# One exponential over two PSUM banks instead of two over one each, and the diagonal key blocks first in the short query chunks, in the second attention of a transformer layer

## The chip, the cores and the metric

The kernel runs as one program on all 8 NeuronCores of one Trainium2 chip. Each core takes one sequence of the batch (4096 tokens of width 1024, float32) and no core talks to another. The time is that of the device, in microseconds, of the slowest core.

## The reference

What is computed, cut to its frame (`layernorm` before each stage, residual added after it):

```python
x = x + attn_a(layernorm(x))      # one head of width 1024, causal, softmax
x = x + ffn(layernorm(x))         # 1024 -> 64, 16 tiny relu units per channel, -> 1024
x = x + attn_b(layernorm(x))      # 16 heads of width 64, causal, then its own layernorm
x = x + ffn(layernorm(x))

# inside attn_b, for every head h
scores = q @ k.T                  # causal: key t is seen by query s only if t <= s
attn = softmax(where(causal, scores / sqrt(64), -inf))
out = attn @ v
```

## The kernel before

The program has four phases with a barrier between them: projections for attention A, attention A with its feed-forward part, projections for attention B (the keys and queries go to HBM, the values stay in SBUF as `v_sb`), and `phase_2b`, attention B with everything behind it. Only `phase_2b` is touched. It runs from about 2526 us to the end at 5371 us.

`phase_2b` works through eight chunks of 512 queries (`qc` 0 to 7). Query chunk `qc` sees `kcnt = 4*qc + 4` blocks of 128 keys (4, 8, ... 32 blocks); the last four of these lie on the diagonal and need a causal mask. In a chunk it goes through eight pairs of heads (`pr` 0 to 7). A head has 64 dimensions, so the two heads of a pair lie on partitions 0 to 63 and 64 to 127.

For every block of keys `kc` at position `pos` of the pair's loop:

- TensorE computes the transposed scores of both heads, 128 keys x 512 queries each, with two matmuls on 64 rows (L1262). They go to two neighbouring banks of `psQ`; `half = pos % 2` chooses banks 0 and 1 or banks 2 and 3. In the text these two are the "score matmuls".
- ScalarE takes the exponential of each head's bank (L1271) into one of three SBUF buffers `AP2[pos % 3]`. Before the change that is one instruction of 512 columns for each head, and the next score matmul on a bank waits only for the exponential that read this bank (`exp_done[(half, hh)]`).
- GpSimd, in the last four blocks only, zeroes what lies above the diagonal, with one `affine_select` for each head (L1280, the "mask"); it waits for both exponentials.
- TensorE multiplies the result with the values, one matmul for each head (L1238), and adds it up in `pc4` and `pc5` over all blocks (the "value matmuls"). These come two positions late in the order of TensorE's queue: scores of `pos`, then values of `pos - 2`. An extra column of ones in `v_sb` gives the sum of the weights in row 64.

After the loop comes the pair's end: Ln and Exp of the sums on ScalarE (L1299 to L1310), two broadcasts by matmul (L1316, L1321), and copies and products on VectorE (L1327 to L1339). The scores of the next pair's positions 0 and 1 are computed meanwhile, the second of them after the end's last VectorE product.

From chunk 1 on, the feed-forward and layernorm work of the chunk before is spread over the pairs by the list `pendf`: its piece `pr` is put into the queues behind the end of pair `pr`, and so runs in front of and beside the loop of pair `pr + 1`. Pieces 0 and 4 are `ep_lnb`: statistics on VectorE (L808, L811), a Ln and an Exp on ScalarE (L825, L828), and then, for each of two row tiles, one scaling (L840) and three adds or products of two SBUF tensors of 128x1024 float32 (L1411, L1414, L1417). Pieces 1 and 5 are statistics and two scalings (L840), pieces 2 and 6 a long chain of small VectorE operations (L903 to L916), pieces 3 and 7 the last matmul of the feed-forward part and, on GpSimd's queue, two stores to `out`. ScalarE's queue is in order, so the exponentials of the next pair stand behind the Ln and Exp of a piece. There is no `pendf` work in chunk 0.

Keys are loaded in pieces of 2048 (16 blocks); `npiece == 1` holds for the chunks with up to 16 blocks, 0 to 3.

Of the kernel before, what the change touches and what calls it, by code (L numbers as in the profile page):

```python
# [8 lines left out]
AF = mybir.ActivationFunctionType  # L9
# [88 lines left out]
def build_nc(debug=False):  # L98
# [27 lines left out]
    p = Prog()  # L126
# [10 lines left out]
    negC = e(nc.sbuf_tensor("negC", [128, 2], F32))  # L137
# [71 lines left out]
    psQ = e(nc.psum_tensor("psQ", [128, 2048], F32))  # L209
# [21 lines left out]
    sm = {n: Sem(e(nc.semaphore(n))) for n in sem_names}  # L231
    PE, DVE, SC, PL = sm["s_pe"], sm["s_dve"], sm["s_sc"], sm["s_pl"]
# [919 lines left out]
    def phase_2b():  # L1152
        exp_done = {}
# [12 lines left out]
        AP2 = [attb2[:, 0:2, :], attb2[:, 2:4, :],  # L1166
               k_sb.ap()[:, 5, 2048:3072].rearrange("p (a b) -> p a b", a=2)]
# [19 lines left out]
        for qc in range(NQ2):  # L1187
            q0 = qc * QC2
            kcnt = 4 * qc + 4
            npiece = (kcnt * 128 + 2047) // 2048  # L1190
# [35 lines left out]
            for pr in range(8):  # L1226
                if pr == 0:
                    issue_k_loads(0)
                def emit_av(kc, pos):
                    for hh in range(2):  # L1230
                        p.wait("tensor", SC, exp_at[kc])
                        if mask_at[kc]:
                            p.wait("tensor", PL, mask_at[kc])
                        if pos == 0:
                            p.wait("tensor", DVE, ctxn_dve[0])
                        h = 2 * pr + hh
                        att = AP2[pos % 3][:, hh, :]
                        p.op("tensor", lambda e_, hh=hh, kc=kc, h=h, att=att, pos=pos, kcnt=kcnt: e_.matmul(  # L1238
                            pb[4 + hh].ap()[0:65, :], v_sbB[:, kc, h, :],
                            att, start=(pos == 0), stop=(pos == kcnt - 1)),  # L1240
                            PE if hh == 1 else None)
# [1 line left out]
                exp_at = {}  # L1243
                mask_at = {}
                pend = []
                order = list(range(kcnt))
                seen_pc = set()
                for pos, kc in enumerate(order):
                    pc = (kc * 128) // 2048
                    koff = kc * 128 - pc * 2048  # L1250
                    half = pos % 2
                    ksl = kslot_of[(qc, pr, pc)]
                    if pc not in seen_pc:
                        seen_pc.add(pc)
                        p.wait("tensor", ksems3[ksl], ktgt[(qc, pr, pc)])
                    if pos == 1:
                        p.wait("tensor", DVE, max(ctxn_dve[0], opj23_free[0]))
                    pe_hh = {}
                    for hh in range(2):
                        bank = pb[2 * half + hh]  # L1260
                        p.wait("tensor", SC, exp_done.get((half, hh), 0))
                        p.op("tensor", lambda e_, b=bank, hh=hh, ks=kslots[ksl], koff=koff, pr=pr: e_.matmul(  # L1262
                            b.ap()[:, :], ks[hh * 64:(hh + 1) * 64, koff:koff + 128],
                            qb2[hh * 64:(hh + 1) * 64, pr, :],
                            start=True, stop=True, tile_position=(hh * 64, 0)), PE)
                        pe_hh[hh] = PE.n
                    for hh in range(2):
                        p.wait("scalar", PE, pe_hh[hh])
                        if pos % 3 == 0 and hh == 0:
                            p.wait("scalar", sm["s_cst"])  # L1270
                        p.op("scalar", lambda e_, ap=AP2[pos % 3], half=half, hh=hh: e_.activation(  # L1271
                            ap[:, hh, :],
                            psQ.ap()[:, half * 1024 + hh * 512:half * 1024 + (hh + 1) * 512],
                            AF.Exp, bias=negC.ap()[:, 1:2]), SC)
                        exp_done[(half, hh)] = SC.n
                    exp_at[kc] = SC.n
                    if kc >= kcnt - 4:
                        p.wait("gpsimd", SC)
                        for hh in range(2):
                            p.op("gpsimd", lambda e_, a_=AP2[pos % 3][:, hh, :], kc=kc, q0=q0: e_.affine_select(  # L1280
                                out=a_, in_=a_,
                                compare_op=ALU.is_ge, fill=0.0,
                                base=q0 - kc * 128, pattern=[[1, QC2]],
                                channel_multiplier=-1), PL)
                        mask_at[kc] = PL.n
                    else:
                        mask_at[kc] = 0
                    if len(pend) == 2:
                        emit_av(*pend.pop(0))
                    pend.append((kc, pos))  # L1290
# [4 lines left out]
                if pr < 7:  # L1295
# [5 lines left out]
                    bias=epsb.ap()[64:65, 2:3]), SC)  # L1301
                p.op("scalar", lambda e_: e_.activation(
                    NORM1[64:65, 0:512], pb[5].ap()[64:65, :], AF.Ln,
                    bias=epsb.ap()[64:65, 2:3]), SC)
# [149 lines left out]
    phase_a(True)  # L1454
    barrier()
    phase_2b()
    p.wait("sync", sm["s_stout"])
    p.wait("sync", sm["s_stx"])
# [56 lines left out]
```

## Time and profile before

| | us |
|---|---|
| median of 2 runs | 5377.53 (5365.68 to 5389.39) |
| the profiled execution | 5372.64 |
| its span on the slowest core (4) | 5371.0 |
| spans of all cores | 5348.1 to 5371.0 |

| engine, core 4 | busy us | share of the span |
|---|---|---|
| PE (TensorE matmul) | 3542.5 | 66% |
| ACT (ScalarE) | 2116.6 | 39% |
| DVE (VectorE) | 1682.5 | 31% |
| POOL (GpSimd) | 524.2 | 10% |

TensorE's granted clock over the whole span is 0.78 on every core; it goes between two levels, 0.5 (1.2 GHz) and 1.0 (2.4 GHz). These shares are means over four phases; the loop that is changed has other limits than the rest. The profile counts an engine as busy while any of its instructions is open, so an instruction that was handed to ScalarE early and waits inside for the one before it counts as busy too, and durations of ScalarE instructions in a dense row overlap. For the pace of such a row one reads the distance from start to start.

### The profile page before, as it was taken

The numbers are of one execution on the slowest core, as the hardware profiler recorded it, in microseconds if no ns is written. First come the engines' busy times: TensorE is split into PE (matmuls) and PEld (weight loads), VectorE is DVE, ScalarE is ACT, GpSimd is POOL, SyncE is SP. The second block draws the span as 40 slices with busy tenths as digits, with TensorE's granted clock in tenths as the row PEclk, the third lists the DMA queues.
The fourth block names the chain that finished last, engine by engine and source line by source line (L and its number), as shares of the span: only waits on it lengthen the run. The fifth ranks groups of instructions, "written<-read, shape, count | busy, mean of one in ns | idle before, by whom it ended". The sixth has DMA issues, their size and how long they took to land.

```text
span 5371.0 us, 49022 instructions; the slowest of 8 cores (5348.1 to 5371.0 us)
## 1 busy us (share of the span) xinstructions
PE 3542.5 (66%) x14217; PEld 1320.0 (25%) x14380; DVE 1682.5 (31%) x3093; ACT 2116.6 (39%) x3829; POOL 524.2 (10%) x916
## 2 busy tenths in 40 slices
PE   1157777567778577776555666677677777777872
PEld 1022222344555322222111111121122122122220
DVE  3222221433222343341144433323322322223126
ACT  0012223222222132222333554546656656757760
POOL 1100000000000010011211111111111001100100
PEclk9978888777888788887566767677788777887875
DMA  8723332111111134343001001010011011010000
GB/s 200 188 102 123 128 122 99 67 59 59 40 40 36 68 112 138 115 138 101 23 21 50 14 27 45 30 39 23 22 41 35 16 43 38 16 39 25 33 20 25
DMA packets 219381, 343.48 MB, mean 64 GB/s; under 512 B 88755, under 2 KB 119475, under 8 KB 219126
## 3 DMA queue, kind: packets, MB, share of 16 engines
q1 hardware_dynamic: 140198, 242.80, 13.7%
q0 software_dynamic: 25552, 80.76, 4.6%
q10 hardware_dynamic: 53376, 16.78, 1.3%
q8 instruction: 128, 2.10, 0.2%
q14 instruction: 127, 1.04, 0.1%
HBM read 260.60 MB, written 75.50 MB: 63 GB/s over the span
## 4 chain that ended last, share of the span: by engine, by line
PE 51%; DVE 18%; issue 9%; ACT 9%; DMA 8%; POOL 3%; DVEq 1%; SPq 0%; ACTq 0%; POOLq 0%
PE pc L1238 9%; PE psQ L684 8%; PE psQ L1262 8%; PE pc L724 5%; ACT arena_b L1271 4%; PE psQ L1068 4%; POOL arena_b L1280 2%; PE pc L1058 2%; PE psQ L1316 2%; DVE stat L811 2%; PE psQ L1321 2%; DVE arena_b L808 1%; DVE k_sb L808 1%; DVE stat L569 1%; ACT k_sb L1271 1%
## 5 line engine op out<-in xcount | busy, mean ns | idle before, releaser
L1271 ACT ACTIVATE arena_b<-psQ,negC 128x512 bf16<-128x512 f32 x1584 | 1003.2, 777 | 414.7 <-PE psQ L1262 357.5
L684 PE MATMUL psQ<-arena_b 128*128 128x512 bf16 x2000 | 567.7, 436 | 150.7 <-ACT arena_b L700 47.1
L1262 PE MATMUL psQ<-arena_b 64*128 64x512 bf16 x1528 | 489.2, 446 | 255.3 <-ACT arena_b L1271 181.8
L1238 PE MATMUL pc<-arena_b,v_sb 128*65 128x512 bf16 x1584 | 560.3, 440 | 108.3 <-POOL arena_b L1280 107.9
L1327 DVE COPY arena_f<-psQ 64x512 f32<-64x512 f32 x64 | 43.7, 682 | 1523.9 <-PE psQ L1316 1523.9
L1271 ACT ACTIVATE k_sb<-psQ,negC 128x512 bf16<-128x512 f32 x720 | 491.5, 790 | 12.3 <-PE psQ L1262 9.5
L1068 PE MATMUL psQ<-arena_b,k_sb 128*128 128x256 bf16 x2176 | 317.6, 296 | 26.4 <-ACT arena_b L1073 19.8
L1280 POOL TENSOR_SCALAR_AFFINE_SELECT arena_b<-arena_b 128x512 bf16<-128x512 bf16 x352 | 210.9, 625 | 1228.0 <-ACT arena_b L1271 1227.6
L1262 PE MATMUL psQ<-arena_b,k_sb 64*128 64x512 bf16 x776 | 248.0, 438 | 123.7 <-ACT arena_b L1271 94.2
L691 ACT ACTIVATE arena_b<-psQ 128x512 bf16<-128x512 f32 x256 | 152.6, 596 | 433.8 <-PE psQ L684 205.3
L724 PE MATMUL pc<-arena_b 128*128 128x512 bf16 x1000 | 251.1, 413 | 102.7 <-DMA arena_b<-wvB_s 53.5
L684 PEld LDWEIGHTS psQ<-arena_b 128*128 128x128 bf16 x2048 | 203.4, 108 | 465.5 <-issue 326.5
L1262 PEld LDWEIGHTS psQ<-arena_b 64*128 64x128 bf16 x1528 | 119.2, 95 | 743.0 <-issue 742.2
L1238 PE MATMUL pc<-k_sb,v_sb 128*65 128x512 bf16 x720 | 249.8, 432 | 44.7 <-POOL k_sb L1280 44.7
L1068 PEld LDWEIGHTS psQ<-arena_b,k_sb 128*128 128x128 bf16 x2176 | 228.8, 106 | 126.7 <-issue 38.7
L825 ACT ACTIVATE stat<-stat,epsb 128x2 f32<-128x2 f32 x48 | 14.2, 295 | 598.8 <-DVE stat L820 598.8
L532 DVE TENSOR_REDUCE nmax<-psQ 1x1 f32<-1x512 f32 x144 | 97.8, 679 | 469.8 <-PE psQ L665 290.7
L1073 ACT ACTIVATE arena_b<-psQ,negC 128x256 bf16<-128x256 f32 x272 | 124.9, 470 | 280.5 <-PE psQ L1068 280.5
L582 ACT ACTIVATE stat<-stat,epsb 128x4 f32<-128x4 f32 x16 | 4.8, 297 | 534.8 <-DVE stat L578 534.8
L1316 PE MATMUL psQ<-arena_f,ones_rowf 1*64 1x512 f32 x128 | 114.6, 993 | 146.5 <-ACT arena_f L1306 146.5
L1238 PEld LDWEIGHTS pc<-arena_b,v_sb 128*65 128x65 bf16 x1584 | 119.6, 117 | 357.9 <-issue 357.9
L1058 PE MATMUL pc<-v_sb,arena_b 128*128 128x512 bf16 x537 | 171.0, 385 | 6.7 <-issue 2.4
(173 smaller groups left out, 4077.0 us busy)
## 6 DMA issues: line engine op xcount, KB each, us to landing
arena_f<-x SPq DMA_DIRECT2D x64, 512.0 KB, 5.9
arena_f<-xs SPq DMA_DIRECT2D x64, 512.0 KB, 5.1
arena_b<-wkT_s SPq DMA_DIRECT2D x16, 1024.0 KB, 7.6
arena_b<-wqT_s SPq DMA_DIRECT2D x16, 1024.0 KB, 6.7
arena_b<-wvT_s SPq DMA_DIRECT2D x16, 1024.0 KB, 6.8
xs<-arena_f POOLq DMA_DIRECT2D x32, 512.0 KB, 3.8
arena_b<-wkB_s SPq DMA_DIRECT2D x16, 1024.0 KB, 7.3
arena_b<-wqB_s SPq DMA_DIRECT2D x16, 1024.0 KB, 7.4
```

The lines of the kernel that those rows point to most:

```text
L684: p.op("tensor", lambda e_, b=bank, ws=wslot, dc=dc, ec=ec: e_.matmul(b.ap()[:, :], wbuf[:, ws, dc % 4, ec * 128:(ec + 1) * 128], lnxT[:, ...
L691: p.op("scalar", lambda e_, b=bank, ec=ec: e_.activation(nsq[:, ec % 2, :], b.ap()[:, :], AF.Square), SC)
L724: p.op("tensor", lambda e_, b=bank, ws=wslot, dc=dc, kt=kt, oc=oc: e_.matmul(b.ap()[:, :], lnxT[:, dc, kt * 128:(kt + 1) * 128], wbuf[:, w ...
L808: p.op("vector", lambda e_, x=x, i=i, stv=stv: e_.scalar_tensor_tensor(junk_ap, x, 1.0, x, ALU.mult, ALU.mult, accum_out=stv[:, 2 + i:3 + ...
L1058: p.op("tensor", lambda e_, att=att, tch=tch, dh=dh, kc=kc, kcnt=kcnt: e_.matmul(AVB[tch][dh], att, v_sb.ap()[:, kc, dh * 512:(dh + 1) * 512],
L1068: p.op("tensor", lambda e_, b=bank, ec=ec, kc=kc, par=par: e_.matmul(b.ap()[:, 0:QS1], k_sb.ap()[:, ec, kc * 128:(kc + 1) * 128], qb1[:, e ...
L1073: p.op("scalar", lambda e_, b=bank, kc=kc: e_.activation(attT1[:, kc, :], b.ap()[:, 0:QS1], AF.Exp, bias=negC.ap()[:, 0:1]), SC)
L1238: p.op("tensor", lambda e_, hh=hh, kc=kc, h=h, att=att, pos=pos, kcnt=kcnt: e_.matmul(pb[4 + hh].ap()[0:65, :], v_sbB[:, kc, h, :], att, s ...
L1262: p.op("tensor", lambda e_, b=bank, hh=hh, ks=kslots[ksl], koff=koff, pr=pr: e_.matmul(b.ap()[:, :], ks[hh * 64:(hh + 1) * 64, koff:koff + ...
L1271: p.op("scalar", lambda e_, ap=AP2[pos % 3], half=half, hh=hh: e_.activation(ap[:, hh, :], psQ.ap()[:, half * 1024 + hh * 512:half * 1024 ...
L1280: p.op("gpsimd", lambda e_, a_=AP2[pos % 3][:, hh, :], kc=kc, q0=q0: e_.affine_select(out=a_, in_=a_, compare_op=ALU.is_ge, fill=0.0, base ...
L1316: p.op("tensor", lambda e_: e_.matmul(pb[2].ap()[0:64, :], ones_rowf.ap()[64:65, 0:64], YT[64:65, 512:1024], start=True, stop=True), PE)
```

## The change

Two edits in the loop over the key blocks of `phase_2b`:

1. The two exponentials of a block, 128x512 each, become one of 128x1024 that reads the two neighbouring banks. It waits for both score matmuls, and both score matmuls of the position two later wait for it (`exp_done[half]`).
2. In the chunks with `npiece == 1` (`qc` 0 to 3) the loop takes the last four blocks, the masked ones, first, and then the others. For chunk 0, which has only these four, the order stays what it was.

The masks, the value matmuls, their count, the pair's end and all other phases stay as they are.

```diff
-                order = list(range(kcnt))
+                if npiece == 1:
+                    order = list(range(max(0, kcnt - 4), kcnt)) + \
+                            list(range(0, max(0, kcnt - 4)))
+                else:
+                    order = list(range(kcnt))
...
+                    p.wait("tensor", SC, exp_done.get(half, 0))
                     if pos == 1:
                         p.wait("tensor", DVE, max(ctxn_dve[0], opj23_free[0]))
-                    pe_hh = {}
                     for hh in range(2):
                         bank = pb[2 * half + hh]
-                        p.wait("tensor", SC, exp_done.get((half, hh), 0))
                         p.op("tensor", ...)            # the score matmul
-                        pe_hh[hh] = PE.n
-                    for hh in range(2):
-                        p.wait("scalar", PE, pe_hh[hh])
-                        if pos % 3 == 0 and hh == 0:
-                            p.wait("scalar", sm["s_cst"])
-                        p.op("scalar", lambda e_, ap=AP2[pos % 3], half=half, hh=hh: e_.activation(
-                            ap[:, hh, :],
-                            psQ.ap()[:, half * 1024 + hh * 512:half * 1024 + (hh + 1) * 512],
-                            AF.Exp, bias=negC.ap()[:, 1:2]), SC)
-                        exp_done[(half, hh)] = SC.n
+                    p.wait("scalar", PE)
+                    if pos % 3 == 0:
+                        p.wait("scalar", sm["s_cst"])
+                    p.op("scalar", lambda e_, ap=AP2[pos % 3], half=half: e_.activation(
+                        ap[:, :, :],
+                        psQ.ap()[:, half * 1024:(half + 1) * 1024], AF.Exp,
+                        bias=negC.ap()[:, 1:2]), SC)
+                    exp_done[half] = SC.n
```

## Rows read from the trace of the kernel before

**Rows 1.** Chain of work that ended last: shares of the span by engine.

```profile
PE 51%; DVE 18%; issue 9%; ACT 9%; DMA 8%; POOL 3%; DVEq 1%; SPq 0%; ACTq 0%; POOLq 0%
```

**Rows 2.** Timeline, ScalarE, chunk 7: start us, length us, engine, line, operation, tiles, count.

```profile
4800.15 2.42 ACT L1271 ACTIVATE arena_b<-psQ,negC 128x512 bf16<-128x512 f32 x4
4802.42 1.30 ACT L1271 ACTIVATE k_sb<-psQ,negC 128x512 bf16<-128x512 f32 x2
4803.56 2.47 ACT L1271 ACTIVATE arena_b<-psQ,negC 128x512 bf16<-128x512 f32 x4
```

**Rows 3.** Timeline, TensorE matmuls, chunk 2, just after the clock rose to 1.0.

```profile
3007.05 0.39 PE L1262 MATMUL psQ<-arena_b,k_sb 64*128 64x512 bf16 x2
...
3007.92 0.39 PE L1262 MATMUL psQ<-arena_b,k_sb 64*128 64x512 bf16 x2
```

**Rows 4.** Timeline, TensorE matmuls, chunk 7, at granted clock 0.5.

```profile
4848.89 0.61 PE L1262 MATMUL psQ<-arena_b 64*128 64x512 bf16 x2
4849.43 1.06 PE L1238 MATMUL pc<-arena_b,v_sb 128*65 128x512 bf16 x2
4850.42 0.61 PE L1262 MATMUL psQ<-arena_b 64*128 64x512 bf16 x2
```

**Rows 5.** Single lines, ScalarE reading PSUM: durations in ns, least/median/most.

```profile
L1271 ACT ACTIVATE arena_b<-psQ,negC x1584: 678/730/1117, 2538.3 to 5214.9; 128x512 bf16<-128x512 f32 x198
```

```profile
L1073 ACT ACTIVATE arena_b<-psQ,negC x272: 452/473/475, 957.6 to 1802.4; 128x256 bf16<-128x256 f32 x136
```

```profile
L1097 ACT ACTIVATE stat<-tb,epsb x16: 252/253/255, 961.6 to 1805.3; 128x1 f32<-128x1 f32 x16
```

**Rows 6.** Stretches, L1271 only: first exponential to L1299's Ln; length, ACT busy, PEclk.

```profile
2595.00:2602.30 7.30, 4.45 (x8) 0.62 0.00 1
2740.50:2755.80 15.30, 9.79 (x16) 0.61 0.01 1
2795.30:2807.90 12.60, 9.70 (x16) 0.74 0.01 1
3062.80:3079.80 17.00, 14.27 (x24) 0.84 0.01 1
3368.60:3390.50 21.90, 19.03 (x32) 0.84 0.00 1
3711.60:3737.90 26.30, 23.51 (x40) 0.89 0.00 1
4952.90:4993.30 40.40, 37.51 (x64) 0.92 0.00 1
```

**Rows 7.** Stretches, all engines: busy PE, PEld, DVE, ACT, POOL; PEclk; DMA share; GB/s.

```profile
4846.00:4853.40 7.40, 6.59 (x16) 1.26 (x16) 6.71 (x8) 6.82 (x12) 0.00 (x0) 0.50 0.00 0
4827.00:4833.00 6.00, 3.04 (x12) 0.70 (x11) 0.00 (x0) 3.65 (x7) 4.63 (x8) 1.00 0.00 0
```

**Rows 8.** Timeline, the last mask and the last value matmuls of a pair.

```profile
4830.69 1.18 POOL L1280 TENSOR_SCALAR_AFFINE_SELECT arena_b<-arena_b 128x512 bf16<-128x512 bf16 x2 [0.24 <-ACT arena_b L1271]
...
4832.01 0.59 PE L1238 MATMUL pc<-arena_b,v_sb 128*65 128x512 bf16 x2 [0.82 <-POOL arena_b L1280]
```

**Rows 9.** Timeline, start of the loop of chunk 1, pair 1.

```profile
2740.52 2.42 ACT L1271 ACTIVATE arena_b<-psQ,negC 128x512 bf16<-128x512 f32 x4
...
2741.04 0.81 DVE L840 TENSOR_SCALAR k_sb<-k_sb,stat 128x1024 f32<-128x1024 f32 x1
...
2741.35 1.16 PE L1262 MATMUL psQ<-arena_b 64*128 64x512 bf16 x2 [6.53 <-ACT arena_b L1271]
...
2741.96 1.23 DVE L1411 TENSOR_TENSOR k_sb<-k_sb,arena_f 128x1024 f32<-128x1024 f32 x1
```

**Rows 10.** Timeline, VectorE, then GpSimd, later in the same loop.

```profile
2748.20 1.44 DVE L1414 TENSOR_TENSOR k_sb<-k_sb,arena_f 128x1024 f32<-128x1024 f32 x1
2749.74 1.44 DVE L1417 TENSOR_TENSOR arena_f<-arena_f,k_sb 128x1024 f32<-128x1024 f32 x1
```

```profile
2747.07 3.04 POOL L1280 TENSOR_SCALAR_AFFINE_SELECT arena_b<-arena_b 128x512 bf16<-128x512 bf16 x2 [11.93 <-ACT arena_b L1271]
```

**Rows 11.** Timeline, GpSimd, masks of chunk 1, pair 3.

```profile
2801.80 1.36 POOL L1280 TENSOR_SCALAR_AFFINE_SELECT arena_b<-arena_b 128x512 bf16<-128x512 bf16 x2 [9.36 <-ACT arena_b L1271]
```

**Rows 12.** Timeline, VectorE, the copy in the end of chunk 1, pair 7.

```profile
2928.39 0.68 DVE L1327 COPY arena_f<-psQ 64x512 f32<-64x512 f32 x1 [3.13 <-PE psQ L1316]
```

**Rows 13.** Timeline, GpSimd, the two stores to `out`, chunk 1, before pair 4's loop.

```profile
2823.32 1.09 POOL L236 DMA_DIRECT2D out<-arena_f  x2 [5.83 <-DVE arena_f L986]
```

## The prediction before the run

> **What bounds the loop now.** I read the chain of waits first. It gives TensorE 51% and ScalarE 9% [rows 1], which would mean that a cheaper exponential buys little. But matmul ends are modelled, so I went by starts. In the middle of a long loop ScalarE starts four exponentials in 4802.42 - 4800.15 = 2.27 us and the next two in 1.14 [rows 2]: one each 0.569 us, without a gap, and 1.14 to 1.155 us for a block. TensorE, right after its clock rose and while it had work saved up, went from one block's score matmuls to the next one's in 3007.92 - 3007.05 = 0.87 us [rows 3]. So at clock 1.0 ScalarE sets the pace. At clock 0.5 the same distance is 4850.42 - 4848.89 = 1.53 us [rows 4], more than ScalarE's 1.14: there TensorE sets it. The stretches by clock show that a loop begins with 7.4 us at 0.5 [rows 7], four to five blocks. With the masks GpSimd is third: two selects take 1.18 us [rows 8].
>
> The stretches from a pair's first exponential to its closing Ln grow from 7.3 us (chunk 0) to 12.6, 17.0, 21.9, 26.3 and 40.4 (chunk 7) [rows 6]. Between Ln and the next pair's first exponential lie the pair's end and the VectorE piece in front of ScalarE's queue; nothing there is changed. VectorE still waits 3.13 us for the pair's end in the tightest kind of pair [rows 12], so it has room for a shorter loop. What a loop loses the kernel therefore loses, once for each of the 64 pairs.
>
> **Edit 1, the joint exponential.** A lone exponential takes at least 678 ns for 512 columns, 452 for 256, and a ScalarE read of one PSUM column takes 253 [rows 5]. The slope is (678 - 253)/511 = 0.83 ns a column (0.88 between 256 and 512). 512 columns are 0.427 us of the 0.569 to 0.577 us pace; some 0.15 us is paid per instruction. One instruction of 1024 columns then has a pace of 0.853 + 0.15 = 1.00 us, and alone takes 0.678 + 0.427 = 1.105. Saved: 0.15 us a block where ScalarE sets the pace. Bounds: with slope 0.88 the fixed part is 0.12 and the saving 0.12; with a fixed part untouched by the overlap (253 ns alone), at most 0.25. I take 0.15, which the dense rows give.
>
> The Trainium skill, "ScalarE: Activation LUTs", section "What ACT_TABLE_LOAD costs", gives 280 ns + 0.833 ns a column with a pointer bias, and 93 ns of overlap between neighbours. By it two pieces cost 1.227 us and one 1.040, a saving of 0.187; the trace has 1.14 to 1.155 for the two, so its fixed part is smaller here. By the page the sum below would be some 25 us larger.
>
> Does the coarser wait cost anything? Scores of position p wait for the exponential of p-2. From its end to the restart of TensorE pass 0.14 us (2740.52 + 0.69 to 2741.35 [rows 9]), the two score matmuls on separate halves of the rows run together in 0.39 us [rows 3], and the exponential follows after some 0.1. That is 0.63 us, inside the 1.00 us of the exponential of p-1. It is hidden; without that cover it would cost up to 0.63 a block.
>
> Chunks 4 to 7: a pair has `kcnt` blocks. About five run at clock 0.5 and gain nothing. The last four pass GpSimd at 1.18 us, so their three gaps gain nothing. About kcnt - 8 gain 0.15, and the last exponential ends (0.585 + 0.68) - 1.105 = 0.16 earlier. (12 + 16 + 20 + 24) blocks x 8 pairs x 0.15 = 86 us, plus 32 x 0.16 = 5: **91 us**.
>
> Chunk 0: four blocks, all masked. The chain mask 0, values 0, scores 3, exponential 3, mask 3, values 3 has two exponentials, each 0.16 shorter: 8 x 0.3 = **2.5 us**.
>
> **Edit 2, masks first, chunks 1 to 3.** Followed from the first exponential at 0, with clock 0.5 to 7 us. Exponential 0 ends at 1.1, mask 0 runs 1.24 to 2.42, values 0 start at 2.56 (0.147 after a mask, as in rows 8: 4831.87 to 4832.01), scores 3 wait behind them until 3.55, values 1 start at 4.1, scores 4 at 5.1, 5 at 6.6. Masks need 1.18 a block and TensorE 1.53, so after the first they are hidden. Then the clock rises, TensorE catches up at 0.87, and ScalarE runs at 1.00 from about block 6 (start 8.4). In chunk 1 block 7 starts at 9.4, ends at 10.5, and its values follow at once; the 1.30 us of the last masks after the last exponential are gone. Ln at 11.35 against 12.6 [rows 6]: 1.25 saved. Chunk 2: Ln at 15.3 against 17.0, 1.7. Chunk 3: 19.4 against 21.9, 2.5. Six of the eight pairs of a chunk: 6 x 5.45 = 33 us. Against it: pair 4 has the two stores ahead of the first mask on GpSimd's queue (1.09 us [rows 13], some 0.6 late, x3), and in pairs 3 and 7 the selects run beside small VectorE operations, 1.36 for two [rows 11] (0.2, x6). Left: **30 us**.
>
> **The price: pairs 1 and 5 of chunks 1 to 3.** Their loops begin beside `ep_lnb`: 0.5 us after the first exponential L840, at 1.4 us the first of three operations with two SBUF inputs, L840, and three more, in all 1.4 + 3 x 1.54 + 0.9 + 3 x 1.54 = 11.5 us with the lengths of [rows 9, 10]. Chunk 1 of before already shows what a select does beside them: two took 3.04 us instead of 1.18, and the VectorE operation 1.44 instead of 1.23 [rows 10]. Before, only the first three selects of such a pair in chunk 1 met the tail of this work (15.3 us to the Ln against 12.6 [rows 6]); in chunks 2 and 3 none did. Now all eight stand in it: mask 0 is ready at 4.2 us, mask 1 at about 6.6, mask 2 at 9.1, mask 3 at 12.0. TensorE's queue is in order, so scores 6 stand behind values 3 and start at 13.1, not at 8. [...] Chunk 1: scores 7 at 14.7, exponential ends 16.5, values 7 at 17.1, Ln at 18.1 against 15.3: +2.8. Chunk 2: two more at 1.53, then 1.0 each, Ln at 22.6 against 17.0: +5.6. Chunk 3: 26.6 against 21.9: +4.7. Two pairs each: **26 us lost**.
>
> The Trainium skill, "SBUF — State Buffer", section "Who interferes with whom", says that a VectorE instruction with two SBUF inputs, or a `tensor_scalar` in a 2-port mode, holds a port that GpSimd needs, and that the later of the two waits for the whole instruction. For the two-input operations the rows agree: one select per operation. For L840 no row shows a select beside it. If it blocks as well, L840 delays the first mask in pairs 1, 2, 5 and 6, and the sum would be some 8 us smaller.
>
> **Sum.** 91 + 2.5 + 30 - 26 = 97 us off the profiled execution's 5372.6. That execution lies 5 us under the median of 5377.5; taken from the median: **5281 us**, 1.8% less. A measurement of this kernel can tell about 2% from no change, which is 107 us here.
>
> **Rivals.**
> - A: the saving is larger. Overlap hides more of a single instruction's fixed cost, or the long VectorE operations and the masks collide less than worked out. Against the latter stands the 3.04 us row [rows 10]. Without any collision pairs 1 and 5 save 11 us instead of losing 26: 97 + 37 = 134 us, 5244. With 0.19 a block, between the 0.15 taken and the bound of 0.25, the 576 blocks of chunks 4 to 7 and some 90 of chunks 1 to 3 give 0.04 x 666 = 27 us more, 5254. Chance 0.22.
> - B: TensorE is the pace, as the chain has it [rows 1]. Then only masks and order count. Of the 5.45 us that edit 2 was given, 15 blocks x 0.15 = 2.3 are edit 1's; 6 x 3.2 = 19 stay, and the sum is 5 + 2.5 + 19 - 3 - 26: no change, 5379. The 0.87 us distance speaks against it. Chance 0.05.
> - C, slower: the clock. Score matmuls that ran apart now run together, and TensorE stands idle longer in each block. Were it no longer held at 1.0, all blocks behind the fifth would take 1.53 instead of 1.15 us: (15+19+23+27) x 8 x 0.38 = 255 us, and 64 us in chunks 1 to 3, near 5700. A microsecond at 0.5 costs 1 - 1.00/1.53 = 0.35; the gain is used up by 280 us more of it, and slower by 2% needs 590. Against it: the clock stayed at 1.0 through 6 us with matmuls busy for 3.04 [rows 7], less than the new loop has. The skill's "TensorE: Matmul & The Clock Gate", "A second HAM failure mode: psum-queue depth-cycling", tells of small idle times between matmuls that made the clock swing; the trace of before shows small gaps at a held 1.0. Chance 0.04.
> - D: the forecast, with its own range 5262 to 5310. Chance 0.69; part of A and of D's low edge falls under 5270.
>
> The range of 8 in 10 is 5245 to 5318: down to A without a collision, up to a saving of 0.12 a block with L840 blocking. Faster by over 2%: 0.26; within 2%: 0.70; slower: 0.04.
>
> **What would show it.** L1271 appears 1152 times as 128x1024 with starts 1.00 us apart at clock 1.0, least duration near 1.10. First exponential to Ln: near 36.6 us in chunk 7, 24.3 in chunk 4, 11.4 in chunk 1. In pairs 1 and 5 of chunks 1 to 3 eight selects over about 11 us, and 18 to 27 us to the Ln. Late score matmuls in mid-loop of chunk 7, a pace over 1.05, or less granted clock there would make the forecast wrong; so would undisturbed masks in those six pairs.

## The result, and the profile after

| | before | after |
|---|---|---|
| median us | 5371.95 (10 runs) | 5264.99 (12 runs) |
| profiled execution, span of the slowest core | 5371.0 | 5260.3 |
| ratio of after to before, undisturbed runs | | 0.9801, 95% interval 0.9776 to 0.9827 |

In some runs one half of the chip shows a lower granted clock and a longer time: the medians count these runs, the ratios (of undisturbed runs) do not.

The change makes the kernel 2.0% faster, some 107 us. The forecast was 97 us less, 5281, in a range of 5245 to 5318. In the profiles the mean span of the eight cores fell by 113.3 us, from 5359.3 to 5246.0.

First the pace, from the timeline of ScalarE and of TensorE's matmuls in the middle of a loop of chunk 7, after (start us, length us, engine, line, operation, tiles, count; core 0). L1272 is the joint exponential, L1265 the score matmul:

```profile
4882.32 2.21 ACT L1272 ACTIVATE arena_b<-psQ,negC 128x1024 bf16<-128x1024 f32 x2
4884.32 1.22 ACT L1272 ACTIVATE k_sb<-psQ,negC 128x1024 bf16<-128x1024 f32 x1
4885.31 2.24 ACT L1272 ACTIVATE arena_b<-psQ,negC 128x1024 bf16<-128x1024 f32 x2
```

```profile
4880.66 0.39 PE L1265 MATMUL psQ<-arena_b 64*128 64x512 bf16 x2
4880.98 0.62 PE L1238 MATMUL pc<-arena_b,v_sb 128*65 128x512 bf16 x2
4881.67 0.39 PE L1265 MATMUL psQ<-arena_b 64*128 64x512 bf16 x2
```

Two exponentials start in 4884.32 - 4882.32 = 2.00 us, the next after 0.99. A block takes 1.00 us against 1.14 before [rows 2]. TensorE's two score matmuls now start together and follow each other at 1.01 us. The row of this line in the profile of single lines gives the time of a lone joint exponential, its least:

```profile
L1272 ACT ACTIVATE arena_b<-psQ,negC x792: 1106/1122/1317, 2542.6 to 5104.8; 128x1024 bf16<-128x1024 f32 x198
```

Next the stretches that answer to [rows 6], from a pair's first exponential to its Ln, after, L1272 alone (stretch, length, busy and count, granted clock, DMA share, GB/s). They are chunk 0; pairs 1 and 3 of chunk 1; pairs 1 and 3 of chunk 2; pairs 1 and 3 of chunk 3; then pair 3 of chunks 4 and 7:

```profile
2598.30:2606.20 7.90, 4.24 (x4) 0.50 0.00 1
2741.70:2759.80 18.10, 8.69 (x8) 0.51 0.00 0
2797.20:2808.30 11.10, 8.44 (x8) 0.70 0.00 0
2998.20:3020.20 22.00, 12.81 (x12) 0.61 0.00 0
3062.90:3078.20 15.30, 12.47 (x12) 0.77 0.01 2
3288.50:3314.50 26.00, 16.83 (x16) 0.67 0.00 1
3359.30:3378.40 19.10, 16.57 (x16) 0.89 0.00 0
3684.40:3708.90 24.50, 20.67 (x20) 0.86 0.00 1
4863.00:4899.30 36.30, 32.69 (x32) 0.92 0.00 1
```

Pair 3 fell from 12.6, 17.0, 21.9, 26.3 and 40.4 us to 11.1, 15.3, 19.1, 24.5 and 36.3. Pair 1 of chunks 1 to 3 rose, from 15.3, 17 and 22 to 18.1, 22.0 and 26.0. The 7.3 us of chunk 0 in [rows 6] can't be set beside the 7.90: that stretch was cut off 0.4 us behind the pair's first exponential and a little ahead of its Ln. The pair in full:

```profile
2594.60:2602.40 7.80, 4.84 (x8) 0.62 0.00 1
```

Over all pairs and cores chunk 0 fell from 8.07 to 7.80 us a pair.

The same length, taken for all 64 pairs on each core, less that of the same pair and core before, summed and averaged over the eight cores (us; negative is faster). "Six pairs" are pairs 1 and 5 of chunks 1 to 3, "clean" the other 18 of these chunks. The last column is what lies between a pair's Ln and the next pair's first exponential.

| kernel | chunk 0 | chunks 1-3, clean | chunks 1-3, six pairs | chunks 4-7 | loops in all | pair ends |
|---|---|---|---|---|---|---|
| forecast | -2.5 | -30 | +26 | -91 | -97 | 0 |
| after (both edits) | -2.1 | -34.7 | +22.7 | -98.8 | -113.0 | -1.2 |
| edit 1 alone | -2.1 | -21.9 | -6.2 | -99.0 | -129.2 | +2.0 |
| edit 2 alone | +0.2 | -12.9 | +26.9 | +0.6 | +14.8 | -13.4 |
| edit 1's waits alone | +0.1 | -0.2 | -0.7 | +0.3 | -0.5 | +1.4 |
| both, pairs 1 and 5 spared | -2.1 | -33.4 | -7.5 | -100.3 | -143.3 | -2.5 |
| all chunks, 1 and 5 apart | -2.1 | -33.0 | -8.0 | -127.4 | -170.5 | -26.1 |
| both, one-input operations | -1.6 | -32.5 | +3.5 | -98.7 | -129.3 | -1.0 |
| both, one score buffer | +12.7 | +124.1 | +48.3 | +620.2 | +805.3 | -3.5 |

What the six pairs look like, from the timelines of GpSimd, of VectorE and of TensorE in chunk 2, pair 1, after (core 0); the loop's first exponential starts at 2998.2:

```profile
2999.47 5.25 POOL L1281 TENSOR_SCALAR_AFFINE_SELECT arena_b<-arena_b 128x512 bf16<-128x512 bf16 x4 [6.59 <-ACT arena_b L1272]
3004.68 2.60 POOL L1281 TENSOR_SCALAR_AFFINE_SELECT k_sb<-k_sb 128x512 bf16<-128x512 bf16 x2
3007.24 3.14 POOL L1281 TENSOR_SCALAR_AFFINE_SELECT arena_b<-arena_b 128x512 bf16<-128x512 bf16 x2
```

```profile
2998.74 0.81 DVE L840 TENSOR_SCALAR k_sb<-k_sb,stat 128x1024 f32<-128x1024 f32 x1
2999.66 1.49 DVE L1412 TENSOR_TENSOR k_sb<-k_sb,arena_f 128x1024 f32<-128x1024 f32 x1
...
3008.46 1.44 DVE L1418 TENSOR_TENSOR arena_f<-arena_f,k_sb 128x1024 f32<-128x1024 f32 x1
```

```profile
3001.77 1.03 PE L1238 MATMUL pc<-arena_b,v_sb 128*65 128x512 bf16 x2 [1.68 <-POOL arena_b L1281]
...
3010.52 1.03 PE L1238 MATMUL pc<-arena_b,v_sb 128*65 128x512 bf16 x2 [1.52 <-POOL arena_b L1281]
3011.49 0.61 PE L1265 MATMUL psQ<-arena_b,k_sb 64*128 64x512 bf16 x2
...
3013.02 0.61 PE L1265 MATMUL psQ<-arena_b,k_sb 64*128 64x512 bf16 x2
...
3014.56 0.61 PE L1265 MATMUL psQ<-arena_b,k_sb 64*128 64x512 bf16 x2
...
3015.78 0.39 PE L1265 MATMUL psQ<-arena_b,k_sb 64*128 64x512 bf16 x2
```

Eight selects, which at the 1.18 us for two of [rows 8] take 4.7 us, take 10.9, from 2999.47 to 3010.38. The value matmuls wait for them, the last masked block's until 3010.52, 12.3 us into the loop, and the next score matmuls stand behind it. TensorE sits in long gaps meanwhile; its matmuls have the length of clock 0.5 (0.61 us) until past 3014 and that of 1.0 (0.39) from 3015.78.

### The profile page after: what moved, and what is told of

Same layout as the page of the kernel before. It is cut to its first block, busy times and chain, and to the rows that moved or that the text cites. A ratio compares the mean times of both kernels' runs of the same rounds, so it can differ in the third digit from the quotient of the medians.

```text
span 5260.3 us, 45857 instructions; the slowest of 8 cores (5228.2 to 5260.3 us)
## 1 busy us (share of the span) xinstructions
PE 3386.8 (64%) x14380; PEld 1276.1 (24%) x14380; DVE 1696.0 (32%) x3093; ACT 1943.1 (37%) x2677; POOL 555.0 (11%) x916
## 4 chain that ended last, share of the span: by engine, by line
PE 40%; DVE 19%; ACT 18%; issue 10%; DMA 8%; POOL 3%; DVEq 1%; SPq 0%; ACTq 0%; POOLq 0%
ACT arena_b L1272 9%; PE psQ L684 9%; PE pc L724 5%; PE pc L1238 4%; ACT k_sb L1272 4%; PE psQ L1068 4%; POOL arena_b L1281 3%; PE psQ L1265 2%; PE psQ L1317 2%; PE pc L1058 2%; DVE stat L811 2%; PE psQ L1322 2%; DVE arena_b L808 2%; DVE k_sb L808 1%; DVE stat L569 1%
## 5 line engine op out<-in xcount | busy, mean ns | idle before, releaser
L1272 ACT ACTIVATE arena_b<-psQ,negC 128x1024 bf16<-128x1024 f32 x792 | 863.7, 1150 | 498.7 <-PE psQ L1265 448.0
L1265 PE MATMUL psQ<-arena_b 64*128 64x512 bf16 x1528 | 347.3, 446 | 298.0 <-ACT arena_b L1272 199.4
L1272 ACT ACTIVATE k_sb<-psQ,negC 128x1024 bf16<-128x1024 f32 x360 | 416.1, 1156 | 27.0 <-PE psQ L1265 26.8
L1281 POOL TENSOR_SCALAR_AFFINE_SELECT arena_b<-arena_b 128x512 bf16<-128x512 bf16 x368 | 246.1, 696 | 1075.1 <-ACT arena_b L1272 1071.6
L1265 PE MATMUL psQ<-arena_b,k_sb 64*128 64x512 bf16 x776 | 175.1, 442 | 145.1 <-ACT arena_b L1272 102.7
L1265 PEld LDWEIGHTS psQ<-arena_b 64*128 64x128 bf16 x1528 | 89.3, 95 | 708.0 <-issue 708.0
```

The costliest lines, as they stand in the source:

```text
L1272: p.op("scalar", lambda e_, ap=AP2[pos % 3], half=half: e_.activation(ap[:, :, :], psQ.ap()[:, half * 1024:(half + 1) * 1024], AF.Exp, bia ...
```

## The experiments

Each was run beside the kernel before on the same chip; "ratio" is its time to that of before, with the 95% interval, as in the first table.

### Edit 1 alone

```diff
-                if npiece == 1:
-                    order = list(range(max(0, kcnt - 4), kcnt)) + \
-                            list(range(0, max(0, kcnt - 4)))
-                else:
-                    order = list(range(kcnt))
+                order = list(range(kcnt))
```

> Edit 1 alone: the joint exponential, key blocks in their old order in every chunk. My theory: the joint exponential is worth 0.15 us for each block that runs at ScalarE's pace, in the short chunks too, and moving the masks to the front gains in 18 pairs and loses in the six pairs beside the layernorm work, so that the second edit adds little or takes away. The profile after shows about 100 us from chunks 4 to 7 and 2 from chunk 0; in chunks 1 to 3 the same saving a block gives (0.3 + 0.8 + 1.3) x 8 = 19 us. Sum 121 us off, about 5251, 14 us faster than both edits together. Rival: the masks at the front carry the gain of chunks 1 to 3 (13 us there with both edits), and the joint exponential alone gives nothing there because the clock is low: then about 102 us off, 5270, slower than both edits.

Ratio 0.9765 (0.9744 to 0.9787), some 126 us. The loops of chunks 1 to 3 lose 28 us (21.9 + 6.2), more than the 19 expected; those of chunks 4 to 7 lose what they lose with both edits. The stretches of chunk 1 pair 3, chunk 2 pair 1, chunk 2 pair 3 (core 6):

```profile
2782.80:2795.10 12.30, 8.58 (x8) 0.76 0.00 0
2990.50:3006.90 16.40, 12.58 (x12) 0.80 0.00 1
3049.10:3065.40 16.30, 12.60 (x12) 0.82 0.01 2
```

Against after, pair 3 is 1.0 to 1.2 us longer and pair 1 of chunk 2 shorter by 5.6.

### Edit 2 alone

```diff
-                order = list(range(kcnt))
+                if npiece == 1:
+                    order = list(range(max(0, kcnt - 4), kcnt)) + \
+                            list(range(0, max(0, kcnt - 4)))
+                else:
+                    order = list(range(kcnt))
```

> Edit 2 alone: two exponentials of 512 columns as before, masked blocks first in chunks 1 to 3. My theory: 18 clean pairs save about 0.8 to 1.0 us each (17 us), the six pairs beside the layernorm work (1 and 5 of each chunk) lose 3, 6 and 6 us (30 us): 13 us slower than before, about 5385, a change of 0.25%. Those six pairs take 18.2, 22.8 and 27.5 us from the first exponential to the Ln. Rival: without the joint exponential the pairs beside the layernorm work are no slower than before, and the edit gains some 20 us, 5352.

Ratio 0.9991 (0.9962 to 1.0019): no difference that the timing can tell. The loops are 14.8 us longer, made of 12.9 us saved in the clean pairs and 26.9 lost in the six (18.2, 22.7 and 27.0 us from first exponential to Ln, as expected). So the rival is out. The pair ends are 13.4 us shorter, which I had not expected, and take most of it back; where that comes from is worked out below, under the masks in all chunks.

### The waits of edit 1 without its instruction

```diff
+                    p.wait("tensor", SC, exp_done.get((half, 1), 0))
                     for hh in range(2):
                         bank = pb[2 * half + hh]
-                        p.wait("tensor", SC, exp_done.get((half, hh), 0))
...
-                        p.wait("scalar", PE, pe_hh[hh])
+                        p.wait("scalar", PE, pe_hh[1])
```

> The waits of edit 1 without its instruction: still two exponentials of 512 columns a block, but both wait for the second score matmul, and both score matmuls of the position two later wait for the second exponential. Order as before. My theory: the coarser waits are hidden behind the exponential of the block between, so the time is that of before within 0.2% (within 10 us), the starts of the exponentials stay 0.57 us apart, and the score matmuls now start together at clock 1.0. All of edit 1's gain is then the saved fixed part of an instruction. Rival: part of the gain comes from the score matmuls that now run together and leave TensorE more room; then this kernel is faster than before by 20 us or more. Third: the coarser wait costs up to 0.6 us a block, and this kernel is slower by up to 500 us.

Ratio 0.9980 (0.9947 to 1.0012); the loops differ by 0.5 us in all. The timelines, chunk 7, core 7:

```profile
4922.02 2.67 ACT L1271 ACTIVATE arena_b<-psQ,negC 128x512 bf16<-128x512 f32 x4
4924.30 1.55 ACT L1271 ACTIVATE k_sb<-psQ,negC 128x512 bf16<-128x512 f32 x2
```

```profile
4921.37 0.39 PE L1262 MATMUL psQ<-arena_b 64*128 64x512 bf16 x2 [0.21 <-ACT arena_b L1271]
4921.69 0.62 PE L1238 MATMUL pc<-arena_b,v_sb 128*65 128x512 bf16 x2
4922.53 0.39 PE L1262 MATMUL psQ<-arena_b 64*128 64x512 bf16 x2 [0.21 <-ACT k_sb L1271]
```

Four exponentials in 2.28 us, as before; the score matmuls start together, TensorE stands idle 0.21 us in every block, and still nothing is gained or lost: 1.16 us a block. ScalarE is the pace, and edit 1's gain is the instruction.

### Both edits, pairs 1 and 5 with their masks last

```diff
-                if npiece == 1:
+                if npiece == 1 and pr not in (1, 5):
```

> Both edits, but pairs 1 and 5 of every chunk keep the old order, masks last. My theory: the six pairs of chunks 1 to 3 in which the masks stood beside operations of VectorE with two SBUF inputs fall from 18, 22 and 26 us back to about 15, 16.5 and 20.7: 27 us less than with both edits, 134 us off before, about 5238. In these pairs of chunks 2 and 3 every select takes 0.61 us again. Rival: these pairs are slow because of other work behind pair 0 and 4, whatever the order of the blocks; then the time stays that of both edits, 5265.

Ratio 0.9746 (0.9695 to 0.9798). The six pairs go from +22.7 to -7.5 us, the others stay. The masks of chunk 2, pair 1 on GpSimd (core 7) have their old pace:

```profile
2995.94 1.18 POOL L1281 TENSOR_SCALAR_AFFINE_SELECT k_sb<-k_sb 128x512 bf16<-128x512 bf16 x2 [15.48 <-ACT k_sb L1272]
2997.07 2.31 POOL L1281 TENSOR_SCALAR_AFFINE_SELECT arena_b<-arena_b 128x512 bf16<-128x512 bf16 x4
```

### Masks away from the end in all chunks

```diff
-                if npiece == 1:
-                    order = list(range(max(0, kcnt - 4), kcnt)) + \
-                            list(range(0, max(0, kcnt - 4)))
-                else:
-                    order = list(range(kcnt))
+                nm = kcnt - 4
+                late = 0 if pr not in (1, 5) else (nm - 3 if nm >= 12 else nm)
+                order = list(range(0, late)) + list(range(nm, kcnt)) + \
+                        list(range(late, nm))
```

> The joint exponential, and masked blocks moved from the end of the loop in all chunks, but not in front of the layernorm work: masks first in pairs 0, 2, 3, 4, 6 and 7 of every chunk; in pairs 1 and 5 masks last in chunks 1 and 2, and from chunk 3 on just ahead of the last three blocks. My theory: what the order edit gains in a clean pair is the mask of the last block between its exponential and its value matmuls, 1.3 us and a little more, whatever the length of the loop. The same 1.45 us a pair in chunks 4 to 7 (24 pairs at the front, 8 ahead of the last three) and in the two pairs of chunk 3 give 34 x 1.4 = 48 us on top of the kernel that spared pairs 1 and 5 (ratio 0.975, 5238): about 5190, ratio 0.966. From the first exponential to the Ln chunk 7 takes 35.1 us against 36.5. Rival: in long loops the masks at the front cost as much as they save, since the start is bound by TensorE at the low clock; then it stays at 0.975. A second one: the last blocks' keys are in the second piece to be loaded and come late; then the first exponentials of chunks 4 to 7 start later and it is slower.

Ratio 0.9635 (0.9600 to 0.9669), median 5169.98 us: 3.6% under before and the fastest kernel of this study. Chunks 4 to 7 lose 28.6 us more than with both edits, or 0.9 us a pair; the expected 1.4 is not reached. From the end of the last exponential to the Ln these pairs are 1.4 us shorter, as expected, but their first six exponentials are spread over 0.7 us more: part of the first rival holds. The rest comes from where nothing was changed: the pair ends are 26.1 us shorter. The row of the first broadcast matmul in a pair's end, among the groups by line, before and then here:

```profile
L1316 PE MATMUL psQ<-arena_f,ones_rowf 1*64 1x512 f32 x128 | 114.6, 993 | 146.5 <-ACT arena_f L1306 146.5
```

```profile
L1316 PE MATMUL psQ<-arena_f,ones_rowf 1*64 1x512 f32 x128 | 97.8, 855 | 146.7 <-ACT arena_f L1306 141.9 <-DVE arena_f L916 4.8
```

It takes 855 ns in the mean instead of 993, and it has two lengths, by the clock it meets. Over the eight cores, before and here, it takes 587 to 729 ns where the granted clock is 1.0 and 704 to 1083 where it is 0.5. Before, 167 of 1008 such matmuls met the 1.0; here 455 of 1002 did, and with edit 2 alone 320 of 1002. Taken apart, the stretch from the first broadcast's start to the second's end is 28.3 us shorter in sum, 216.9 to 188.6, while what lies before it and just behind it changed by under 1 us. So the shorter ends come from the clock. Why more ends meet the higher clock is argued: the loop no longer ends in waits for masks, so the broadcasts come sooner after dense matmuls. No run forced the clock.

### One SBUF input instead of two

```diff
-                    p.op("vector", lambda e_, y=y: e_.tensor_tensor(
-                        y[:, :], y[:, :], gamB[:, :], ALU.mult), DVE)
+                    p.op("vector", lambda e_, y=y: e_.tensor_scalar(
+                        y[:, :], y[:, :], 1.0, None, ALU.mult), DVE)
```

and the same for the two adds behind it.

> Both edits, and in the layernorm piece the six operations of VectorE with two SBUF inputs are replaced by scalings with one input of the same 128x1024 float32 size. It leaves out gamma, beta and the residual add of attention B. My theory: the selects of pairs 1 and 5 are slow because the operations beside them have two SBUF inputs and are long; with one input a select is held only for a short time (0.43 us in all beside two L840 in pair 2 of the kernel after), and VectorE is through sooner (0.91 us instead of 1.44 an operation). Eight selects take 5.5 to 7 us in sum instead of 11.2, the six pairs fall by 2 to 5 us each, some 20 to 25 us in all: ratio about 0.975. Rival: any VectorE operation of this size holds GpSimd for its whole length, one select for each; then the sum is 8 x 0.9 = 7.2 us with the last select near 8.5 us, and half of the loss stays. Second rival: the selects are slow for another reason (their own queue, the buffers): the sum stays 11.2 us and the time that of both edits.

Ratio 0.9733 (0.9699 to 0.9768). The six pairs go from +22.7 to +3.5 us. GpSimd and VectorE in chunk 1, pair 1 (core 6):

```profile
2729.47 3.65 POOL L1281 TENSOR_SCALAR_AFFINE_SELECT arena_b<-arena_b 128x512 bf16<-128x512 bf16 x4 [6.62 <-ACT arena_b L1272]
2733.08 2.07 POOL L1281 TENSOR_SCALAR_AFFINE_SELECT k_sb<-k_sb 128x512 bf16<-128x512 bf16 x2
```

```profile
2729.66 0.96 DVE L1412 TENSOR_SCALAR k_sb<-k_sb 128x1024 f32<-128x1024 f32 x1
2730.73 0.91 DVE L1415 TENSOR_SCALAR k_sb<-k_sb 128x1024 f32<-128x1024 f32 x1
```

Two selects now take 2.07 us instead of 3.1, still not 1.18, and the scalings 0.91 instead of 0.81. It is the first rival of this run that holds: GpSimd gets through one select for each operation of VectorE, whether that has one input (1.01 us apart) or two (1.55 us apart). My own theory, that one input would leave the selects nearly alone, falls. What the two inputs add is length (1.44 against 0.91 us), and so the time of each turn. Against the kernel that spares these pairs (-7.5 us), 11 of 30 us of the loss are left; the rival had said half.

### The two halves of psQ no longer overlapped

```diff
-                    p.wait("tensor", SC, exp_done.get(half, 0))
+                    p.wait("tensor", SC, max(exp_done.get(0, 0), exp_done.get(1, 0)))
```

> Both edits, but the score matmuls of a position wait for the exponential of the position right before, so that the two halves of psQ no longer overlap. My theory: this lays bare the ring that the prediction called hidden: exponential 1.105, restart of TensorE 0.14, score matmuls 0.39 (0.61 at clock 0.5), hand-over 0.1: 1.74 us a block at clock 1.0 and 1.95 at 0.5, instead of 1.00 and 1.53. Some 770 blocks x 0.74 and 320 x 0.42 give 700 us more, about 5965. TensorE then works some 0.64 us of matmul columns in 1.74 us. If the clock holds at 1.0 with so little work, the rival of the prediction that lets the clock fall in the denser loop of both edits is far off; if the clock falls, the pace is 1.95 throughout and the time nearer 6150.

6170.11 us, ratio 1.1498 (1.1457 to 1.1540): near the second of the two cases, 6150. TensorE's matmuls and the stretch around them, chunk 7, core 4 (busy PE, PEld, DVE, ACT, POOL, granted clock):

```profile
5902.17 0.61 PE L1265 MATMUL psQ<-arena_b 64*128 64x512 bf16 x2 [0.37 <-ACT arena_b L1272]
5902.71 1.06 PE L1238 MATMUL pc<-k_sb,v_sb 128*65 128x512 bf16 x2
5904.14 0.61 PE L1265 MATMUL psQ<-arena_b 64*128 64x512 bf16 x2 [0.37 <-ACT arena_b L1272]
```

```profile
5860.00:5900.00 40.00, 32.57 (x82) 6.43 (x80) 0.00 (x0) 22.93 (x21) 0.00 (x0) 0.50 0.00 0
```

A block takes 5904.14 - 5902.17 = 1.97 us, the ring worked out for clock 0.5 (1.95). The clock stays at 0.5 over the whole stretch, with a wait of 0.37 us in each block. So it was nearly everywhere: the loops ran at 0.5 for 2309 of their 2360 us, in the mean of the cores. But it could rise. In four of the 512 loops it rose in the middle and then stayed at 1.0 for 20 us; in the others no stretch at 1.0 was longer than 3.4 us. Core 4, chunk 5, pair 2, TensorE across the rise, which is at 4377.54:

```profile
4376.04 0.61 PE L1265 MATMUL psQ<-arena_b 64*128 64x512 bf16 x2 [0.36 <-ACT arena_b L1272]
...
4378.01 0.39 PE L1265 MATMUL psQ<-arena_b 64*128 64x512 bf16 x2 [0.36 <-ACT arena_b L1272]
...
4379.76 0.39 PE L1265 MATMUL psQ<-arena_b 64*128 64x512 bf16 x2 [0.81 <-ACT k_sb L1272]
```

There a block takes 4379.76 - 4378.01 = 1.75 us, the 1.74 of the first case, though TensorE now waits 0.81 us in each. The overlap that the prediction called a cover for the coarser wait is worth 905 us (6170.11 - 5264.99, against the kernel with both edits, of which this is the only change). Of the 0.97 us that it costs a block in mid-loop, 0.75 are the ring at clock 1.0 and the other 0.22 the lower clock.

### Both edits and edit 1 alone, side by side

No edit; the two kernels again, beside each other and the kernel before.

> The changed kernel itself once more, to set it beside the joint exponential alone on one chip. Theory: the second edit as it was made costs more in the six pairs beside the layernorm work (2 x (2.8 + 5 + 4.5), about 25 us) than it gains in the 18 others; in the profiles the loops of chunks 1 to 3 lose 10 to 14 us with both edits and 28 with the joint exponential alone. Then this kernel is 10 to 15 us slower than the joint exponential alone. Rival: the difference of the two ratios (0.9801 and 0.9765) is scatter between the calls, and side by side they are the same within 5 us.

> Edit 1 alone once more, beside both edits. Theory: ratio 0.975 to 0.978, lower than both edits by 0.002 to 0.003. Rival: equal ratios.

Ratios 0.9805 (0.9740 to 0.9870) and 0.9841 (0.9768 to 0.9915): with intervals this wide neither answer is excluded, and the ratios don't settle which of the two is faster. The loops do agree with the first profiles: 113.5 and 128.0 us less than before in the mean, and no core of one kernel lies among those of the other (109.5 to 117.6 against 122.3 to 133.2). The spans say the same, if halves of the chip (the median of four cores) are taken at the granted clock of each kernel's first profile: 5242.8 to 5252.5 us with both edits (eight halves, clock 0.774 to 0.776), 5225.6 to 5232.4 with edit 1 alone (five halves, 0.780 to 0.782). So edit 1 alone is the faster kernel, by some 16 us.

## Why the prediction was right, point by point

**Which engine is the pace.** Right: the chain's 51% for TensorE was no guide, the starts were. Rival B, no gain from the exponential, is out by edit 1 alone (0.9765), and the run with the waits alone shows that changes to TensorE's order within a block move nothing.

**The price of the joint exponential.** 1.105 us alone and 1.00 in a row were forecast; 1.106 and 1.00 were measured. A straight line through 1 and 512 columns held at 1024, over two banks.

**The cover of the coarser wait.** Right, and shown twice: the waits alone cost nothing, and without the overlap the ring has the length that was added up, at either clock (1.97 and 1.75 us against 1.95 and 1.74).

**Chunks 4 to 7.** 98.8 us against 91, which is nearer than its parts. Summed over the distances from start to start of these 32 pairs, in the mean of the cores: the 544 between the sixth block and the first masked one gave 77.3 us, 0.142 each, where 576 x 0.15 = 86 had been forecast. The first five of each pair gave 6.3 and the three among masked blocks 9.4, both of which I had put at nothing. The last exponential and the way to the Ln gave 5.8, for 5. That masked blocks gain nothing was wrong: before, their starts lie 1.14, 1.14 and 1.72 us apart, after 1.00, 1.00 and 1.72. Only the last waits for the masks. So 9 us too many in the middle hid over half of the 16 left out at the edges, and that is luck.

**Chunk 0.** 2.1 us against 2.5. Right, although the row of 7.3 us was cut short.

**Edit 2 in the clean pairs.** The 34.7 us with both edits are near the 30 forecast, but its parts were off both ways. By the sums under rival B some 14 of the 30 were edit 1's and 16 the order's. Edit 1 brings 21.9, and the order 12.8 (34.7 - 21.9; 12.9 when alone). The mask that is gone from the end is worth more than forecast: the way from the last exponential's end to the Ln is 25.7 us shorter in these 18 pairs, 1.43 each for 1.30. But the first five distances between starts, which now hold the masks, are 14.0 us longer in sum and take that much back.

L840 does hold the selects: in chunk 1, pair 2, two of them delay four selects by 0.4 us, from 2.31 to 2.75. By the rule of the Trainium skill, "SBUF — State Buffer", section "Who interferes with whom", the text had put 8 us on twelve pairs, 0.7 each. The direction is the rule's, the size smaller. The one-input run fits the rule too, if its scalings run in the 2-port mode that the page asks for; no run here shows in which mode they ran.

**The six pairs.** +22.7 us against +26; the profile showed it pair by pair (18.1, 22.0 and 26.0 us to the Ln, forecast 18.1, 22.6 and 26.6). Sparing them removes it. One term of the hand sum had no row: after block 7 it let two more blocks go by at 1.53 us before the pace of clock 1.0. In chunk 2, pair 1, the starts after block 7 are 3014.56 - 3013.02 = 1.54 and 3015.78 - 3014.56 = 1.22 us apart, and 0.87 from there on. It follows that edit 2 as made costs 29 us in six pairs (22.7 + 6.2) for 12.8 gained in eighteen; the loops are 16 us shorter without it.

**The pair ends.** Put at nothing; with both edits they measured -1.2 us. It need not have come so: with edit 2 alone and with the masks moved in all chunks they lost 13.4 and 26.1 us.

**The clock.** Rival C did not come: from 4870 to 4895 us, in mid-loop of chunk 7, the granted clock is 1.0. But the row that I held against it showed only a clock that stays up through a thin stretch. Whether it rises from 0.5 in the first place is another question, and with one buffer it seldom did: in four loops of 512. How near the changed kernel is to that no run shows.

## What to carry to other kernels

Where ScalarE reads PSUM in a dense row, one instruction over two banks saves the fixed part of the second, 0.14 us a block here, as long as two such pairs of banks alternate. Before moving work of one engine to another place in time, look up what the neighbours of its port do there: masks that took 0.6 us each at the end of a loop took 1.4 at its start in six pairs. And judge a loop's reordering also by what comes behind it: of the 197 us that the best kernel's loops and pair ends lost, 26 lie in code that nobody touched.

## What the runs showed of the hardware that I had not expected

- A one-input scaling of 128x1024 float32 on VectorE (0.81 us alone, 0.91 beside GpSimd) holds GpSimd's selects as an add of two tensors does: one select for each, 1.01 us apart against 0.57 for selects alone (four in 2.31 us).
- With matmuls idle 0.37 us in every 1.97, TensorE's granted clock stayed at 0.5 for 98% of the loops' time, on core 4 for 645 us without a break. In four loops of 512 it rose, and then stayed at 1.0 for 20 us with TensorE idle 0.81 us in every 1.75. In the run with edit 1's waits alone a loop whose TensorE stands idle 0.21 us in every 1.16 kept the 1.0.
